# Second layer norm folded into the attention loop of a fused attention and mixture-of-experts layer, shared network started at the loop's end, expert offsets computed by matmuls

## What is computed

```python
x = x + tanh(g_xattn) * attention(layernorm(x), ctx, ctx, frac)   # bias from clip(frac_k - frac_q, -0.2, 0.2)
x = x + tanh(g_ffn) * ffn(layernorm(x))
...
# ffn, on 2048 tokens of 256
logits = xf @ gate_w + gate_b
top_w, top_i = top_k(logits, 2); gw = softmax(top_w)
out = sum over the 2 chosen experts e of gw * (gelu(xf @ w1[e] + b1[e]) @ w2[e] + b2[e])
shared = gelu(xf @ ws1 + bs1) @ ws2 + bs2
return out + shared
```

## Time and profile before

| | us |
|---|---|
| median of 3 runs | 588.13 |
| the 3 runs | 588.13, 589.6, 580.5 |
| profiled execution, its own time | 587.57 |
| its span | 585.7 |

### The profile page before, as it was taken

How to read it: one execution, slowest core, us unless ns; L and a number is a source line. 1 busy time by engine, 2 the same in 40 slices (tenths; PEclk the granted TensorE clock), 3 DMA queues, 4 the chain that set the end, 5 groups by cost and what they waited for, 6 DMA issues and landing times.

```text
span 585.7 us, 17314 instructions
## 1 busy us (share of the span) xinstructions
PE 516.2 (88%) x6424; PEld 421.7 (72%) x6425; DVE 408.1 (70%) x972; ACT 309.3 (53%) x722; POOL 262.1 (45%) x193
## 2 busy tenths in 40 slices
PE   2698699899999997599679999999999999999990
PEld 0354477777777776456346668899999999999990
DVE  4965648787878788969848748666666666666660
ACT  3656546666666665468336665444544544444430
POOL 4344527575757653459566624322323323323322
PEclk9889969999999999879798999999999999999996
DMA  9500012233323341134253685322223233222121
GB/s 278 199 1 5 1 41 88 65 106 120 96 69 102 118 130 37 41 105 139 87 172 126 197 179 186 66 45 54 38 51 54 36 53 54 36 54 53 28 29 18
DMA packets 37554, 49.17 MB, mean 84 GB/s; under 512 B 8066, under 2 KB 30722, under 8 KB 37380
## 3 DMA queue, kind: packets, MB, share of 16 engines
q1 hardware_dynamic: 30356, 39.18, 22.5%
q0 software_dynamic: 7152, 9.34, 8.7%
HBM read 31.79 MB, written 16.72 MB: 83 GB/s over the span
## 4 chain that ended last, share of the span: by engine, by line
PE 64%; DVE 23%; ACT 4%; DMA 3%; issue 3%; POOL 1%; SPq 0%; POOLq 0%; DVEq 0%; ACTq 0%
PE bank L1172 59%; DVE mx L830 4%; DVE W L840 3%; PE bank L1270 3%; DVE W L805 2%; PE bank L1433 1%; ACT W L627 1%; DVE m L833 1%; DMA xres<-x 1%; DVE xres L861 1%; DVE hbuf L960 1%; DVE st L863 1%; DVE xres L812 1%; DMA xres<-xs_dram 1%; POOL rstd L444 1%
## 5 line engine op out<-in xcount | busy, mean ns | idle before, releaser
L762 ACT ACTIVATE hbuf<-bank,b1t 128x128 f32<-128x128 f32 x312 | 88.7, 368 | 112.2 <-PE bank L1172 109.6
L1172 PE MATMUL bank<-W,xT 128*128 (+1 forms) x1704 | 136.5, 249 | 0.4 <-DVE xT L1128 0.4
L1172 PE MATMUL bank<-xres,W 128*128 128x128 bf16 (+1 forms) x1920 | 124.7, 224 | 9.5 <-DVE xres L812 9.2
L563 POOL DMA_INDIRECT out<-xres,idu x39 | 60.7, 1557 | 156.3 <-DVE xres L1147 147.2
L1172 PEld LDWEIGHTS bank<-xres,W 128*128 (+1 forms) x1920 | 111.9, 98 | 18.6 <-issue 8.8
L1172 PEld LDWEIGHTS bank<-W,xT 128*128 128x128 bf16 (+1 forms) x1704 | 113.9, 97 | 14.4 <-issue 1.0
L1172 PE MATMUL bank<-W 128*128 128x17 bf16 (+3 forms) x1440 | 86.2, 207 | 3.2 <-DVE W L840 1.5
L1172 PEld LDWEIGHTS bank<-W 128*128 128x128 bf16 x1440 | 67.8, 98 | 16.6 <-DVE W L840 2.7
L487 POOL TENSOR_TENSOR W<-stage,W 128x1024 bf16<-128x1024 f32 x28 | 60.6, 2167 | 39.8 <-ACT W L619 31.8
L1172 PE MATMUL bank<-W,hsplit 128*128 128x256 bf16 x432 | 57.3, 283 | 9.3 <-DVE hsplit L1089 5.5
L1172 PEld LDWEIGHTS bank<-W,hsplit 128*128 128x128 bf16 x432 | 43.7, 102 | 24.1 <-DVE hsplit L1089 6.2
(11 more groups left out here) (153 smaller groups left out, 662.7 us busy)
## 6 DMA issues: line engine op xcount, KB each, us to landing
stage<-wts SPq DMA_DIRECT2D x36, 512.0 KB
xres<-xs_dram SPq DMA_DIRECT2D x39, 128.0 KB, 2.1
xs_dram<-hbuf SPq DMA_DIRECT2D x7, 645.0 KB, 6.5
W<-ctxT SPq DMA_DIRECT2D x4, 512.0 KB, 6.0
xres<-x SPq DMA_DIRECT2D x4, 512.0 KB, 7.9
out<-xres SPq DMA_DIRECT2D x4, 512.0 KB, 5.3
W<-wproj SPq DMA_DIRECT2D x4, 256.0 KB, 6.8
hsplit<-frac SPq DMA_DIRECT2D x16, 64.0 KB, 5.8
```

Source lines behind the costliest of these rows:

```text
L563: nc.gpsimd.indirect_dma_start(out, bass.IndirectOffsetOnAxis(idu[:, par, t:t + 1], axis=0), ysb[par][t], None, compute_op=ALU.add).then_i ...
L762: ins = nc.scalar.activation(hbuf[:, q, c * TR:(c + 1) * TR], bank[UPS * par + q][:, c * TR:(c + 1) * TR], ACT.Gelu, bias=b1t[:, par, UC * ...
L1172: return nc.tensor.matmul(o, a, b, start=start, stop=stop, **kw)
```

## The change

In the attention core, per image: in the odd slot of image b DVE makes `stats2(b - 2)`, which stood in the even slot, `aggregate2(b - 2)` and `inputs2_low(b - 3)`, the low part of the normalised and transposed rows; POOL makes `deviation2(b - 2)`, four small instructions; ACT normalises image b - 3 (`norm2`, even slot) and makes its high part (`inputs2_high`, odd slot); PE transposes it (`turn2`, two transposes, odd slot). The transposed rows pass through the upper half of bank 7, where `project_o` also writes, so there are waits between them. Images 13 to 15 follow in the first steps of the shared network (`last_tokens`).

PE starts `shared_up(0)` right behind `project_o(14)`. The gate of images 0 to 11 is one block of 96 matmuls behind `shared_up(1)`, the others follow at m = 1, 2 and 3. The matmuls of the mask stand at m = 6 (`RANKS_AT`): 16 that sum up the count of every expert, one with `upb`, and 15 that add the images before; DVE is left with 7 small instructions in place of the running sums. POOL makes the low parts to m = 9.

Pieces: the first 16 in the core, 4 on POOL at m = 4 to 7, 12 on DVE (`LOWS_AT`), and the last 4 on POOL in tiles 0 to 3. ACT makes the high part of each of these 4 behind `gelu_tile` and `high_tile` of that tile, and SP issues their loads behind `store_group(3)` and the load of b2; PE asks for them at tile 16. Four tiles are unrolled in place of two, and the loop is in two parts.

```diff
-POOL_PIECES_AT = (1, 3, 4, 6, 7)
-VECTOR_PIECES = range(PIECES - 12, PIECES - 4)
-HIGHS_AT = (10, 11, 13, 15, 18, 20, 22, 23)
-LOWS_AT = (11, 12, 14, 16, 19, 21, 23, 24)
-LAST_HIGHS_AT = (28, 30)
+POOL_PIECES_AT = (4, 5, 6, 7)
+VECTOR_PIECES = range(NOW + 4, PIECES - 4)
+HIGHS_AT = (10, 11, 13, 14, 16, 17, 19, 20, 22, 24, 26, 28)
+LOWS_AT = (11, 12, 14, 15, 17, 18, 20, 21, 23, 25, 27, 29)
-POOL_SPLITS = HC
+POOL_SPLITS = 10
+RANKS_AT = 6
+UP_BANKS = (0, 1, 6)
+EARLY_TOKENS = B - 4
...
@@ sync
+            load_pieces(NOW, NOW + 7)
             store_group(0)
+            load_pieces(NOW + 7, NOW + 11)
             store_group(1)
+            load_pieces(NOW + 11, PIECES - 4)
...
             sp.dma_start(b2f, b2.to_broadcast([P, E * D])).then_inc(ld_b2, 16)
-            with sp.Fori(2, TILES // 2) as i:
+            load_pieces(PIECES - 4, PIECES - 2)
+            load_tile(4, 0)
+            load_piece(PIECES // 2 - 1, 0)
+            load_tile(5, 1)
+            load_piece(PIECES // 2 - 1, 1)
+            with sp.Fori(3, TILES // 2) as i:
...
@@ gpsimd
+            def deviation2(b):
+                pool.wait_ge(ln2_stat, b + 1)
+                link(inverse_deviation(rstd2, mv2, b, b + 1))
+                link(nc.gpsimd.tensor_tensor(nmr2[:, b:b + 1], mv2[:, b:b + 1, 0], rstd2[:, b:b + 1], ALU.mult))
+                nc.gpsimd.tensor_scalar(nmr2[:, b:b + 1], nmr2[:, b:b + 1], -1.0, None, ALU.mult).then_inc(ln2_rstd, 1)
...
-                if b < B - 1:
-                    piece_low(b // 2, b % 2)
+                piece_low(b // 2, b % 2)
+                if b >= 2:
+                    deviation2(b - 2)
...
@@ scalar
+            def norm2(b):
+                act.wait_ge(ln2_rstd, b + 1)
+                if b:
+                    act.wait_ge(x2T_ps, b)
+                nc.scalar.activation(xh2, xres[:, b * D:(b + 1) * D], ACT.Identity,
+                                     scale=rstd2[:, b:b + 1], bias=nmr2[:, b:b + 1]).then_inc(xh2_ready, 1)
...
             def body(j, par, more):
                 gelu_tile(j, par)
                 if more == 2:
                     high_tile(j + 2, par)
+                if isinstance(j, int) and j < 4:
+                    piece_high((PIECES - 4 + j) // 2, j % 2)
...
@@ vector, slot(u)
                 if u % 2 == 0 and b >= 2:
                     residual(b - 2)
-                if u % 2 == 1 and b >= 1:
-                    outputs_low(b - 1)
+                if u % 2 == 1:
+                    if b >= 2:
+                        stats2(b - 2)
+                    if b >= 1:
+                        outputs_low(b - 1)
+                    if b >= 2:
+                        aggregate2(b - 2)
+                    if b >= 3:
+                        inputs2_low(b - 3)
...
@@ tensor
+            def turn2(b):
+                pe.wait_ge(xh2_ready, b + 1)
+                if b >= B - 3:
+                    pe.wait_ge(x2_lo, b)
...
+            def ranks():
+                pe.wait_ge(sel_ready, 1)
+                sel = selm.rearrange("p b e -> p (b e)")
+                for b in range(B):
+                    mm(bank[4][:, B * E:(B + 1) * E], oneb[:], sel[:, b * E:(b + 1) * E], b == 0, b == B - 1)
+                mm(bank[4][:, 0:B * E], upb[:], sel, True, False, skip_group_check=True)
+                for b in range(1, B):
+                    ins = mm(bank[4][:, b * E:B * E], oneb[:], sel[:, 0:(B - b) * E], False, b == B - 1, skip_group_check=True)
+                ins.then_inc(rank_ps, 1)
```

More of the change, by code:

```diff
@@ L282, in wait_alone, with tiles @@
             eng.sem_inc(passed[name], 1)
[L284 to L288, removed]
+        def tiles(eng, body, late=None):
+            for j in range(4):
+                body(j, j % 2, 2)
+            with eng.Fori(2, LATE_TILES // 2) as i:
+                body(2 * i, 0, 2)
+                body(2 * i + 1, 1, 2)
+            if late:
+                late()
+            with eng.Fori(LATE_TILES // 2, TILES // 2 - 1) as i:
                 body(2 * i, 0, 2)
@@ L565, in add_tile @@
                         ysb[par][t], None, compute_op=ALU.add).then_inc(added[t], 16)
-            add_tile(0, 0)
-            add_tile(1, 1)
-            with pool.Fori(1, TILES // 2) as i:
+            for j in range(4):
+                piece_low((PIECES - 4 + j) // 2, j % 2)
+                add_tile(j, j % 2)
+            with pool.Fori(2, TILES // 2) as i:
                 add_tile(2 * i, 0)
@@ L997, in _, with choose @@
-            link(ins)
+            output(B - 1)
+            residual(B - 2)
+            stats2(B - 2)
+            aggregate2(B - 2)
+            outputs_low(B - 1)
+            inputs2_low(B - 3)
+            residual(B - 1)
+            stats2(B - 1)
+            aggregate2(B - 1)
+            inputs2_low(B - 2)
+            def choose(lo, hi):
+                dve.wait_ge(gate_ps, hi)
+                link(nc.vector.tensor_tensor(lg[:, lo:hi], gate_bank(lo)[:, lo * E:hi * E].rearrange("p (b e) -> p b e", e=E),
+                                             row[:, V_GB:V_GB + E].rearrange("p (o e) -> p o e", o=1).to_broadcast([P, hi - lo, E]),
+                                             ALU.add))
+                for b in range(lo, hi):
+                    ins = nc.vector.max(mx8[:, b, :], lg[:, b, :])
+                link(ins)
+                for b in range(lo, hi):
+                    ins = nc.vector.max_index(ix8[:, b, :], mx8[:, b, :], lg[:, b, :])
+                return ins
@@ L1374, in w_up, with last_tokens @@
+            def last_tokens(m):
+                if m == 0:
+                    project_o(B - 1)
+                    turn2(B - 2)
+                if m == 1:
+                    pe.wait_ge(x1_ready, B)
+                    gate(EARLY_TOKENS, B - 2)
+                if m == 2:
+                    turn2(B - 1)
+                    gate(B - 2, B - 1)
+                if m == 3:
+                    gate(B - 1, B)
+                if m == RANKS_AT:
+                    ranks()
             def w_up(base, part, c, j):
@@ L1439, in _ @@
             shared_up(1)
+            turn_o(B - 1)
+            turn2(B - 3)
+            gate(0, EARLY_TOKENS)
             for m in range(HC * GROUPS):
```

268 lines of the change are left out of this document (108 added, 160 removed).

## The result

The changed kernel takes **603.8 us** (median of 4, 602.2 to 604.4) where the kernel before takes 585.5 on the same chip (median of 4, 580.5 to 589.6). The ratio is 1.034, with an interval of 1.025 to 1.043: slower, where I forecast 582. The profiled execution is 603.35, its span 601.5, against 585.7 before.

The account below looks back on a forecast made before the run. PE was taken to bound the core, late network and tiles (busy over 90%), leaving gains in the second norm and early shared network; +9 - 19.1 - 2.3 + 3 + 4 = -5.4 on 587.57 gave 582 us, range 571 to 592.

Parts of the forecast that it names:

- Core: +9: Attention core: moved work lengthens each image by 0.7 us, +9 us in all, bounds +6 and +12.
- the upper bound: Core, +12 us: POOL's deviation delays `split_difference` past the next scores, some tenths twelve times, the last 3 us.
- my first rival: Core doesn't lengthen: DVE's additions are covered, only PE's transposes remain at 12 x 0.2, time 575; chance 0.24.
- the slow rival: Core: PE's longer waits cost it full clock, two images at half clock make 600, 2% slower; chance 0.05.
- my signs of being wrong: Core images of 9.8 us, or 11 and more with PE waiting for `split_difference`; ACT waiting for pieces, m = 11 to 29.
- the term for the choice of experts: `shared_up(0)` to `shared_down(10)`: -2.3 us, from 37.9 of PE work plus 1 for blocked DVE instructions, against 41.2; bounds -5, +4.
- Second norm, -19.1: The second norm as its own stage goes: 19.34 us saved, less 0.2 for a delayed `project_o(14)`.
- The rest of the network, +3: `shared_down(10)` to the network's end: DVE's extra work at m = 10 costs +2.5, later +0.5; bounds -4 and +8.
- The unnamed loss of 7.4: Rest of the network: 7.4 us lost before the change, mostly ACT waiting for nothing the profile names; assumed to stay.
- transfers bound the network: Rest of the network: pairs of pieces wait for landing, +8 us, 592 with a later tile start; chance 0.16.
- The tiles, +4 to +7: Tiles: ACT waits for late piece 32 behind the first gelu, +4 us, up to +7 with lost PE clock.
- POOL's low parts hide: Tiles: POOL's low parts of the last pieces cost nothing, since POOL only waits there.

Follow-up runs that it names:

- e2: The changed kernel with the reductions writing bf16 peaks directly, both small DVE instructions on the peaks removed: 578.1 us, ratio 0.994.
- e3: The kernel before the change, with the same edit as e2 (peaks reduced straight into bf16, no small instructions): 570.6 us, ratio 0.981.
- e12: e2 with POOL's deviation moved behind the next `split_difference`: 572.2 us.
- e8: The changed kernel with the edits of e2 and e4, and the gather of payload rows begun at network step 12 rather than 10: 572.8 us.
- e14: The changed kernel with all winning edits (e2, e4, e9's low parts on DVE, e12's late deviation), payload rows from step 11: 562.1 us, ratio 0.967.
- e16: e14 with the loads of the last 16 pieces cut to 128 of 1024 columns: 557.4 us.
- e17: e14 with DVE's low parts of twelve late pieces replaced by zero times the high part: 557.8 us.
- e19: e14 with both cuts together, those of e16 (loads) and e17 (low parts): 560.2 us, ratio 0.956.
- e4: The changed kernel with the loads of pieces 32 and 33 issued ahead of the last two stores and the tiles' loads: 597.8 us.
- e9: e8 with the low parts of the last four pieces made on DVE instead of POOL, six tiles unrolled instead of four: 568.9 us.
- e18: e3 run again, in the series of e16 and e17: 569.1 us, ratio 0.980.

## Why the prediction was wrong

The failed step is **"Core: +9"**, measured +23.9. It costs the halves of an image at 4.65 and 5.75, as the work that moves in and out of a loop otherwise unchanged; they came out at 5.48 and 6.19. The loop did change: DVE's first small instruction on the peaks, 0.27 and 0.49 in the trace of the kernel before (none of my rows shows it), became 1.28 and 1.16, because it waits for POOL's instruction beside it. Without it the change costs 0.62 per image and not 1.95 (e2, e3).

- *What was near by luck.* My 0.7 per image for DVE's added work meets the 0.62 of e2 against e3, but 0.36 of that is POOL's deviation ahead of `split_difference`, which I had put into the upper bound. With the deviation late (e12) the added work costs 0.26 in that loop, near the 0.2 for PE's transposes of my first rival: there PE waits for DVE at neither `turn_peaks`, so DVE's 1.0 is covered. What that 1.0 costs by itself in the loop with the small instructions, no run separates.
- *What was right in it.* The clock didn't fall (0.97), so the slow rival that I priced at 0.05 wasn't the one that came. Of my signs of being wrong, the image of 11 and more came, but PE waited for DVE's peaks and not for `split_difference`; ACT's waits for pieces came too.
- *What was missing.* I moved POOL's deviation and checked `split_difference` only against its reader, PE's scores. That check was about right: in e2 it is late by 0.19. I didn't ask which DVE instructions POOL's would now lie beside. With 0.27 and 0.49 taken as lengths, there was nothing to ask.
- *The rule I had in hand.* In the term for the choice of experts I weighed the Trainium skill (SBUF — State Buffer, Terms), by which DVE and GpSimd share a port pair that one of them holds for a full instruction, and disputed only how often it would strike there. In that place the sum was near by luck: the stretch came to -2.6 for my -2.3, but PE's work was 35.7 us where I had 37.9, and its waits 2.9 where I allowed 1. The seven small instructions took 4.0 us (284.08 to 288.12), where I had 1.9 and 1; one of eight columns alone took 1.74. The place for the rule was the core, in 26 of 32 slots. There the trace agrees with the blocking by the ends of the instructions, to 0.04 us; it also shows that reductions from a bank, and the statistics, aren't held.
- *Second norm, -19.1*: -19.3, right.
- *The rest of the network, +3*: +5.4, and both halves of the reasoning failed. The unnamed loss of 7.4, which I kept, isn't there in the profile after; the new waits are some 12 (66.1 for 53.3 of work). DVE's pile of 5.1 at step 10 was there and a wait of 3.70 for a scatter with it, which I hadn't seen: the payload of step 10 reuses the slot of the first. But e8 shows that this wait isn't the cause of the length. Of the 11.1 between e14's rest and e3's, 2.6 come back when the loads of the late pieces are cut and 3.8 when their low parts are (e16, e17), the first of them hardly more than the scatter of the stretch. That the two add up isn't shown, as e19 failed to tell; even if they do, what holds the other 5 stays open. The rival "transfers bound the network" is true in part at most.
- *The tiles, +4 to +7*: +8.4. The late load of piece 32 was right (e4 gives back 6.8 of the stretch). "POOL's low parts hide" was the same error as in the core: they hold DVE's splits for up to 3.8, worth another 3 (e9).

Of 21.8 us between 582 and 603.8, the core has 15, the tiles 4.4, the rest of the network 2.4. The forecast also started from an execution of the kernel before with the unnamed loss; against the 581 of other series the changed kernel's 603.8 is 23 slower, not 18.

## What to carry to other kernels

When a step on one engine is moved, list what runs beside it on the other engine at the new time, and look at the ends: where a small instruction ends with its neighbour's, its length in the profile is a remainder, and will be another after the move. A small instruction on SBUF operands that sits in a loop of four engines can be worth making part of one that reads a bank, even when it looks like 0.2 us: here that gave 10.5 us without the change and 25.7 with it. And the largest wait in a late stretch isn't yet its cause: take it away once, as e8 does, before building on it.

## What the runs showed of the hardware that was not expected

- A DVE instruction of 8 columns between SBUF operands took 0.17 us alone and mostly 1.16 to 1.29 beside GpSimd's in the changed kernel's core, once 2.03 (114.31), to within 0.04 of its neighbour's end. DVE reductions of a bank took 1.27 to 1.28 for two in either case, and the statistics of 256 columns in SBUF 0.43.
- The clip's second instruction on GpSimd (2.07 us, two operations on 128x512) is an exception: DVE's small one began under it at 72.64 and 99.33 in the changed kernel and at 72.68 in the kernel before, and ended each time 0.78 after the clip's had begun, 1.3 before that one's end.
- In the tiles a cast of 512 columns took 3.31 in place of 0.42 and ended 0.3 behind GpSimd's subtraction, though its record begins 0.28 before that one's. GpSimd's scatter (381.21 to 382.83) was still running then, and the subtraction's record of 2.72, in place of 2.13, reaches back over it: from the scatter's end it is 2.16. So these rows don't show that GpSimd lost time.
- GpSimd's deviation of one column took 1.43 from its first instruction to the next step (178.08 to 179.51), against 1.92 for four columns; the power alone is 0.57.
- The unnamed gaps come and go: in the shared network ACT has two in the profile of the kernel before (3.25 and 6.25 us, PE stopping beside the second), two in e19, none in e3, e18, e14 or the changed kernel. One packet of the queue "instruction" lies in the 6.25 of the kernel before, none in either gap of e19; e3, e14 and the changed kernel have such packets in that stretch and no gap (at 289.9, 291.0 and 297.2). The Trainium skill (Runtime: NRT & Kernel Launch, Instruction fetch mechanics) has each engine fetch its code in blocks by DMA; these rows neither show nor rule out that the gaps are such fetches, and their cause stays open.
